# A five-stage graph network on one core: the three dense stages rewritten as one interleaved pass, with centred weights and a bias added by TensorE

## The chip, the cores and the metric

The kernel runs on one core of one Trainium2 chip. The metric is the device time of one execution in microseconds (us); lower is better. A difference is given against the median of the runs of the kernel before.

## What is computed

The reference chains two graph layers, a mixture of experts, a third graph layer and a block that modulates the better half of the tokens, on 6250 nodes with 256 features and 100000 edges, all in fp32:

```python
def _gnn_layer(x, row, col, W, b, g, beta):          # layers gnn0 and gnn1
    agg = segment_sum(x[col], row); deg = maximum(segment_sum(1, row), 1)
    h = (x + agg / deg) @ W.T + b
    mu = mean(h, -1); var = mean(square(h - mu), -1)
    return silu((h - mu) * rsqrt(var + EPS) * g + beta)

updated = x @ W_self.T + b_self + aggregate @ W_msg.T + b_msg     # layer gnn2
out = gelu(layernorm(updated) * ln_gamma + ln_beta)
```

After gnn1 and gnn2 the result is added to the residual `x`, and the sum is normalised again.

## The kernel before

The program is a list of stages, each a block in which the five engines have queues of their own and meet through semaphores; the next stage starts when all are through. The order is: `sort` (edges sorted by node through a table in DRAM), `sum0`, `gnn0`, `sum1`, `gnn1`, `route`, `moe_in`, `moe`, `moe_out`, `sum2`, `gnn2`, `half`. The nodes are held in SBUF as 49 tiles of 128 rows (NT = 49, D = 256, U = 7 tiles to a loop iteration, KB = 2 blocks of 128 columns): `p.acc` has the sums over edges and then the new rows, `p.xb` the rows before the layer.

`sum_over_edges` (L730) gathers the neighbours' rows by indirect DMAs on the POOL queue (L888) and adds them per node by one-hot matmuls (L956) and VectorE adds (L1118). In `sum2` it also makes `x @ W_self.T + b_self + b_msg` beside the gathers and puts it into `p.xb`.

`gnn_dense` (L1267) is the dense stage, built three times: `gnn0`, `gnn1` and `gnn2`. It has two passes over the 49 tiles. The first is class `Project` (L1132). Per tile VectorE makes the rows (`put`, L1280, a copy at L1282 in gnn2) four tiles ahead, TensorE transposes them with the identity (L1197, two matmuls) two tiles ahead, ScalarE copies the transposed rows out of PSUM (L1226), TensorE multiplies by the weights (L1212, two fp32 matmuls, which the trace shows as four records), VectorE adds the bias or `p.xb` on the way out of PSUM (`take`, L1286) and collects row statistics (`norm.take`, L568). Then `norm.finish` (L570 to L586) turns the statistics of all 49 tiles into mean and reciprocal deviation, with one square root by ScalarE (L629). The second pass is `tile` (L1325): per tile VectorE subtracts the mean and multiplies by gamma (`center`, L1315), multiplies by the deviation and adds beta (`scale`, L1321), ScalarE applies Silu or Gelu (L1366), and where there is a residual VectorE adds it (L1335) and takes the statistics of the sum (L568). Each loop iteration of ScalarE's second pass holds one ACT_TABLE_LOAD. In gnn0 the result is sent to DRAM by SyncE, seven tiles to a DMA (`send_steps`).

The edges' second table, which `sum2` reads, is written by 784 indirect DMAs on the POOL queue (`Scatter.run`, L1256). They are spread over three stages: columns 0 to 97 beside gnn0 (`EC // 8` = 98), 98 to 195 beside gnn1, and 196 to 783 beside `moe`. A stage that has scatters can't end before they are issued and landed.

Of the kernel before, what the change touches and what calls it, by code (L numbers as in the profile page):

```python
# [24 lines left out]
P = 128  # L25
N = 6250
D = 256
# [702 lines left out]
def sum_over_edges(p, source, order, weighted, table, own=None):  # L730
# [4 lines left out]
    with ExitStack() as ctx:  # L735
# [18 lines left out]
        s_landed, s_free = s("s_landed"), s("s_free")  # L754
        if own is not None:
# [82 lines left out]
        def _(act):  # L838
            if table is not None:
# [13 lines left out]
                clear(early, at)  # L853

# [407 lines left out]

def second_scatter(p, ctx):
    return Scatter(p, ctx, p.table1, p.addr1, p.rec1)


def gnn_dense(p, wk, mean_of_edges, row_bias, gamma, beta, func, residual, copy, scatters, left=None):  # L1267

    nc, v = p.nc, p.nc.vector
    with ExitStack() as ctx:
        deg = p.sb("g_deg", [P, NT], F32, ctx)
        norm, norm2 = RowNorm(p, ctx), left or RowNorm(p, ctx)

        def put(t, slots):
            a, x = flat(p.acc[:, bass.ds(t, 1), 0:D]), flat(p.xb[:, bass.ds(t, 1), :])
            if mean_of_edges:
                return [v.scalar_tensor_tensor(out=slots[0], in0=a, scalar=deg[:, bass.ds(t, 1)], in1=x,  # L1280
                                               op0=ALU.mult, op1=ALU.add)]
# [19 lines left out]
        block = ctx.enter_context(nc.Block())  # L1301

        @block.vector
        def _(dve):
# [16 lines left out]

            center(0, 0)
            center(1, 1)  # L1325
            scale(0, 0)

            def tile(t, u, more):
                x = flat(p.acc[:, bass.ds(t, 1), 0:D])
# [957 lines left out]
```

## Time and profile before

| what | us |
|---|---|
| three runs | 7439.2, 7442.39, 7440.92 (median 7440.92) |
| the profiled execution, its own time | 7400.07 |
| its span | 7398.1 |
| TensorE busy, share of the span | 49% |
| VectorE busy | 38% |
| ScalarE busy | 11% |
| GpSimd (POOL) busy | 51% |

In the profile PE is TensorE's matmuls, PEld its weight loads, DVE VectorE, ACT ScalarE, POOL GpSimd and SPq SyncE's queue. Times in the trace are microseconds from the span's start. A matmul in fp32 against the weights stands there as two records, a transposition as one. PEclk is the share of full speed that TensorE's clock was granted; 1.00 is 2.4 GHz and 0.50 is 1.2 GHz. The bracket at the end of a row of the timeline is how long the engine was idle before it, and what the profile gives as the releaser.

### The profile page before, as it was taken

To read this page: it belongs to the slowest core of one execution; us is meant where nothing else is said; L and a number is where in the kernel's file an instruction comes from. 1 tells how busy PE (TensorE), PEld (TensorE's weight loads), DVE (VectorE), ACT (ScalarE), POOL (GpSimd) and SP (SyncE) were. 2 spreads that over 40 slices of the span, in tenths; PEclk is the share of its full clock that TensorE was granted. 3 is DMA by queue.
4 is the path that set the end of the run, shared out by engine and by line. 5 is a ranking of instruction groups with operands and counts; after the bars stand their busy time and mean duration, and the time that the engine had idled before them with its cause. 6 is when DMAs were issued, how large, how long until landed. Compare 5 with 4: busy or idle time off the path is not lost. (4 is left out here: it accounts for less than half of the span.)

```text
span 7398.1 us, 63577 instructions
## 1 busy us (share of the span) xinstructions
PE 3606.4 (49%) x13693; PEld 2603.5 (35%) x13694; DVE 2823.8 (38%) x6837; ACT 831.4 (11%) x2066; POOL 3772.0 (51%) x3797
## 2 busy tenths in 40 slices
PE   4113965444433445445331222299992455555529
PEld 1001543333322333333230000078881344344317
DVE  5116854444435344444380000011114455555761
ACT  0001930000002000000130000022221100000222
POOL 4772046666662666666507777700005566667221
PEclk7556987777766777777655555599996777778759
DMA  3001023333311333332012000022214333333140
GB/s 134 1 0 37 13 58 92 93 92 91 92 42 47 92 91 93 92 93 84 5 38 91 2 4 4 9 72 81 81 57 135 90 91 92 90 90 92 55 160 18
DMA packets 290129, 497.38 MB, mean 67 GB/s; under 512 B 99253, under 2 KB 182880, under 8 KB 290048
## 3 DMA queue, kind: packets, MB, share of 16 engines
q0 software_dynamic: 163264, 345.19, 16.5%
q1 hardware_dynamic: 125696, 150.28, 6.3%
q10 hardware_dynamic: 1088, 1.05, 0.1%
q8 instruction: 25, 0.41, 0.0%
q14 instruction: 56, 0.46, 0.0%
HBM read 487.50 MB, written 92.89 MB: 78 GB/s over the span
## 5 line engine op out<-in xcount | busy, mean ns | idle before, releaser
L956 PE MATMUL sum_sums<-sum_got,sum_onehot 128*128 x4992 | 1627.4, 487 | 1717.5 <-DVE acc L1118 1317.3
L888 POOL DMA_INDIRECT sum_got<-xn,edge_row x1568 | 1539.5, 982 | 1139.8 <-issue 450.4
L956 PEld LDWEIGHTS sum_sums<-sum_got,sum_onehot 128*128 128x128 f32 x4992 | 1173.7, 245 | 2153.5 <-issue 1944.0
L1118 DVE TENSOR_TENSOR acc<-acc,sum_sums 128x257 f32 (+1 forms) x2496 | 1053.2, 422 | 1775.8 <-remote 1242.6
L888 POOL DMA_INDIRECT sum_got<-h,edge_row x784 | 753.9, 962 | 484.0 <-issue 226.3
L1256 POOL DMA_INDIRECT table<-rec,addr x784 | 807.8, 1030 | 291.5 <-issue 275.4
L1763 PE MATMUL moe_f_ps_y<-xb,moe_f_hT 128*128 128x256 f32 x1792 | 475.9, 398 | 297.7 <-issue 297.6
L1747 PE MATMUL moe_f_ps_h<-moe_f_xT,xb 128*128 128x256 f32 x1792 | 473.7, 398 | 286.5 <-issue 286.3
L1828 DVE TENSOR_TENSOR moe_f_y<-moe_f_ps_y,moe_b 128x256 f32<-128x256 f32 x112 | 42.3, 420 | 1337.2 <-PE moe_f_ps_y L1763 650.1
L1595 POOL DMA_INDIRECT moe_out_c_got<-moe_out,place_i x98 | 95.7, 976 | 826.2 <-PEq L1553 787.9
L1256 POOL DMA_INDIRECT table<-sort_rec,sort_addr x392 | 400.4, 1022 | 202.1 <-issue 122.5
L1763 PEld LDWEIGHTS moe_f_ps_y<-xb,moe_f_hT 128*128 128x128 f32 x1792 | 349.8, 197 | 391.6 <-issue 351.3
L1747 PEld LDWEIGHTS moe_f_ps_h<-moe_f_xT,xb 128*128 128x128 f32 x1792 | 352.9, 199 | 366.3 <-issue 324.7
L1075 DVE TENSOR_TENSOR sum_onehot<-iota,edge_local 128x512 f32<-128x512 f32 x636 | 435.4, 685 | 6.0 <-PEq L2246 6.0
L1795 ACT ACTIVATE moe_f_hT<-moe_f_ps_h,moe_b 128x256 f32<-128x256 f32 x448 | 187.9, 470 | 1365.4 <-remote 788.5
L310 PE MATMUL sort_placed<-acc 128*128 128x392 f16 x1576 | 264.1, 331 | 39.4 <-DVE acc L528 37.0
L1222 ACT ACTIVATE gnn_pr_spare<-eps 128x1 f32<-128x1 f32 x9 | 1.2, 193 | 2319.2 <-PEq L2246 2319.2
L252 ACT ACTIVATE acc<-acc,edge_row 128x128 f16<-128x128 f16 x784 | 256.2, 392 | 8.7 <-DVE acc L538 5.8
L1543 POOL DMA_INDIRECT moe_in<-xb,place_i x98 | 95.5, 975 | 257.2 <-DVE xb L609 227.6
L310 PEld LDWEIGHTS sort_placed<-acc 128*128 128x128 f16 x1576 | 154.6, 98 | 148.9 <-issue 39.3
L342 PE MATMUL sort_placed<-sort_mask,sort_before 128*128 128x392 f16 x168 | 68.6, 408 | 229.8 <-issue 149.8
L1197 PE MATMUL gnn_pr_psflip<-ident,gnn_pr_rows 128*128 128x128 f32 x294 | 67.1, 319 | 229.3 <-issue 137.4
(481 smaller groups left out, 3432.2 us busy)
## 6 DMA issues: line engine op xcount, KB each, us to landing
xb<-in_L_ffn_W SPq DMA_DIRECT2D x112, 1024.0 KB
sum_got<-xn,edge_row POOLq DMA_INDIRECT x1568
moe_in<-acc SPq DMA_DIRECT2D x28, 512.0 KB
moe_f_xin<-moe_in SPq DMA_DIRECT2D x56, 256.0 KB
moe_out<-moe_f_y SPq DMA_DIRECT2D x56, 256.0 KB
xn<-xb SPq DMA_DIRECT2D x14, 896.0 KB
table<-rec,addr POOLq DMA_INDIRECT x784
sum_got<-h,edge_row POOLq DMA_INDIRECT x784
```

Source lines behind the costliest of these rows:

```text
L252: nc.scalar.activation(hot[:, j, CH + part * P:CH + (part + 1) * P], hot[:, j, CH + 2 * P:CH + 3 * P], ACT.Copy, scale=value[:, bass.ds(n, ...
L310: mm = nc.tensor.matmul(placed[part][:, half, 0:CH // 2], hot[:, slot, CH + part * P:CH + (part + 1) * P], hot[:, slot, half * (CH // 2):( ...
L888: pool.indirect_dma_start(got[:, c % SU, 0:D], None, source, bass.IndirectOffsetOnAxis(ap=p.edge_row[:, c:c + 1], axis=0)).then_inc(s_got[ ...
L956: mm = nc.tensor.matmul(sums[k % 2][j], onehot[:, (k % QUARTERS) * HALF + j, :], flat(got[:, bass.ds(where[n % PLAN], 1), :]), start=True, ...
L1075: ins = v.tensor_tensor(out, number, local, ALU.is_equal)
L1118: v.tensor_tensor(a, a, sums[k % 2][j], ALU.add).then_inc(s_added[j], 1)
L1256: pool.indirect_dma_start(self.table, bass.IndirectOffsetOnAxis(ap=self.addr[:, c:c + 1], axis=0), self.rec[:, c, :], None, bounds_check=l ...
L1543: pool.indirect_dma_start(into[0:places, :], bass.IndirectOffsetOnAxis(ap=p.place_i[:, k, t:t + 1], axis=0), p.xb[:, t, :], None, bounds_c ...
L1595: pool.indirect_dma_start(got[:, t % U, k, :], None, source, bass.IndirectOffsetOnAxis(ap=p.place_i[:, k, t:t + 1], axis=0)).then_inc(s_go ...
L1747: mm = nc.tensor.matmul(ps_h[j // 2][:, j % 2, :], w1[:, wk, kb, j * P:(j + 1) * P], xT[:, k, kb, :], start=(kb == 0), stop=(kb == KB - 1))
L1763: mm = nc.tensor.matmul(ps_y[k][:, blk, :], hT[:, k, j, blk * P:(blk + 1) * P], w2[:, wk, j, :], start=False, stop=(j == HB - 1 and blk == 1))
L1795: nc.scalar.activation(hT[:, k, j, :], ps_h[j // 2][:, j % 2, :], func, bias=bias).then_inc(s_act, 1)
```

## The change

1. In `sum0` ScalarE, after it has cleared the sums, takes from each of the eight blocks of weights in `p.wT` and from four bias rows its mean over the 256 output columns (12 activations with an accumulated sum, one that divides by -256, and 12 that add the result). With centred weights and bias the projected row has mean zero. `sum1` and `sum2` have nothing of this.
2. `gnn_dense` is one interleaved pass, written out for all 49 tiles without loops. The bias row (gnn0, gnn1) or `p.xb` (gnn2) is added by TensorE: one more fp32 matmul per tile, with the identity as the weights and the row as the 256 moving columns. The variance comes from ScalarE, by a Square of the PSUM rows with scale 1/16 and an accumulated sum. VectorE's `center`, its first statistics and the copy of gnn2's rows are gone; its `take` multiplies by gamma. The square root is taken per group of seven tiles, and scale, activation and residual sum follow 9, 10 and 12 tiles behind.
3. The split of the scatters is 0 to 71 beside gnn0, 72 to 167 beside gnn1 and 168 to 783 beside `moe`.

```diff
+            for n, columns_of in enumerate(centre):
+                nc.scalar.activation(columns_of, columns_of, ACT.Copy, accum_out=middle[:, n:n + 1]).then_inc(s_totals, 1)
...
+            for n, columns_of in enumerate(centre):
+                nc.scalar.activation(columns_of, columns_of, ACT.Identity, bias=middle[:, n:n + 1]).then_inc(s_centred, 1)
...
+FEW, MOST = 72, 168
+BANKS, FLIPS, PUTS = 4, 2, 4
+SCALE_LAG, ACTIVE_LAG, SUM_LAG = 9, 10, 12
...
+        @block.tensor
...
+            for t in range(NT):
+                if t + FLIPS < NT:
+                    turn(t + FLIPS)
+                out = ps_out[t % BANKS][:, 0:D]
+                if t >= BANKS:
+                    pe.wait_ge(s_taken, t - BANKS + 1)
+                nc.tensor.matmul(out, p.ident[:], row_bias[:] if mean_of_edges else p.xb[:, t, :], start=True, stop=False)
+                pe.wait_ge(s_copied, t + 1)
+                for kb in range(KB):
+                    last = nc.tensor.matmul(out, flip[:, t % U, kb * P:(kb + 1) * P], p.wT[:, wk, kb, :], start=False,
+                                            stop=(kb == KB - 1))
+                last.then_inc(s_out, 1)
...
+        @block.scalar
...
+            for n in range(NT + ACTIVE_LAG):
+                if n + FLIPS < NT:
+                    keep(n + FLIPS)
+                if n < NT:
+                    act.wait_ge(s_out, n + 1)
+                    if n >= 2:
+                        act.wait_ge(s_square, n - 1)
+                    nc.scalar.activation(squares[:, n % 2, :], ps_out[n % BANKS][:, 0:D], ACT.Square, scale=1.0 / 16,
+                                         accum_out=std[:, n:n + 1]).then_inc(s_square, 1)
...
+                    nc.scalar.activation(out, scaled[:, t % U, :], func).then_inc(s_active, 1)
+                if n < NT and n % U == U - 1:
+                    act.wait_ge(s_square, n + 1)
+                    nc.scalar.activation(std[:, group(n // U)], std[:, group(n // U)], ACT.Sqrt,
+                                         bias=p.eps[:, 0:1]).then_inc(s_std, 1)
...
+        @block.vector
...
+            for n in range(NT + (SCALE_LAG if residual is None else SUM_LAG)):
+                if n < NT:
+                    dve.wait_ge(s_square, n + 1)
+                    v.tensor_tensor(p.acc[:, n, 0:D], ps_out[n % BANKS][:, 0:D], gamma[:], ALU.mult).then_inc(s_taken, 1)
+                    if mean_of_edges and n + PUTS < NT:
+                        put(n + PUTS)
...
-              row_params["L0_gnn_beta0"], ACT.Silu, None, dram["h1"], (0, EC // 8))
+              row_params["L0_gnn_beta0"], ACT.Silu, None, dram["h1"], (0, FEW))
-              row_params["L0_gnn_beta1"], ACT.Silu, io["x"], None, (EC // 8, EC // 4))
+              row_params["L0_gnn_beta1"], ACT.Silu, io["x"], None, (FEW, MOST))
-              (io["L0_ffn_W1"], io["L0_ffn_W2"], p.moe_b1, p.moe_b2), True, ACT.Gelu, (EC // 4, EC))
+              (io["L0_ffn_W1"], io["L0_ffn_W2"], p.moe_b1, p.moe_b2), True, ACT.Gelu, (MOST, EC))
```

TensorE's queue in gnn0, the first pass in the loop. Before, one tile is two transpositions (`psflip`) and two matmuls with the weights (`psout`); each `psout` row is two records of the trace:

```order
L1197 MATMUL gnn_pr_psflip<-ident,gnn_pr_rows 128x128
L1197 MATMUL gnn_pr_psflip<-ident,gnn_pr_rows 128x128
L1207 REGISTER_ALU
L1212 MATMUL gnn_pr_psout<-wT,gnn_pr_flip 128x256
L1212 MATMUL gnn_pr_psout<-wT,gnn_pr_flip 128x256
```

In the change it is:

```order
L1329 MATMUL gnn_g_psflip<-ident,gnn_g_mixed 128x128
L1329 MATMUL gnn_g_psflip<-ident,gnn_g_mixed 128x128
L1341 MATMUL gnn_g_psout<-row_L_gnn_b,ident 128x256
L1344 MATMUL gnn_g_psout<-wT,gnn_g_flip 128x256
L1344 MATMUL gnn_g_psout<-wT,gnn_g_flip 128x256
```

The third row, the bias times the identity, is new; it stands between the transposition two tiles ahead and the tile's own product.

ScalarE's queue in gnn0 of the change, around the end of a group of seven tiles (L1354 the copy of the transposed rows, L1365 the Square, L1376 Silu, L1379 the square root of a group):

```order
L1354 ACTIVATE gnn_g_flip<-gnn_g_psflip 128x256
L1365 ACTIVATE gnn_g_squares,gnn_g_std<-gnn_g_psout 128x256
L1376 ACTIVATE xb<-gnn_g_scaled 128x256
L1379 ACT_TABLE_LOAD
L1379 ACTIVATE gnn_g_std<-gnn_g_std,eps 128x7
L1354 ACTIVATE gnn_g_flip<-gnn_g_psflip 128x256
L1365 ACTIVATE gnn_g_squares,gnn_g_std<-gnn_g_psout 128x256
L1376 ACT_TABLE_LOAD
L1376 ACTIVATE xb<-gnn_g_scaled 128x256
```

Before, the copies, the root and Silu lay one after the other, with one table load per seven tiles; now they alternate, and a group has two.

VectorE's queue in gnn1, second pass before (one tile), and one step of the change (L1407 `take`, L1398 `put`, L1419 scale, L1425 the residual sum):

```order
L1321 SCALAR_TENSOR_TENSOR gnn_pr_flip<-gnn_g_centered,gnn_n6rstd,row_L_gnn_beta 128x256
L1335 TENSOR_TENSOR acc<-gnn_g_active,gnn_pr_rows 128x256
L1315 ISA
L1315 SCALAR_TENSOR_TENSOR gnn_g_centered<-acc,gnn_n6mean,row_L_gnn_g 128x256
L568 ISA
L568 BN_STATS gnn_n7stats<-acc 128x6
```

```order
L1407 TENSOR_TENSOR acc<-gnn_g_psout,row_L_gnn_g 128x256
L1398 SCALAR_TENSOR_TENSOR gnn_g_mixed<-acc,gnn_g_deg,xb 128x256
L1419 SCALAR_TENSOR_TENSOR gnn_g_scaled<-acc,gnn_g_std,row_L_gnn_beta 128x256
L1425 TENSOR_TENSOR acc<-gnn_g_active,gnn_g_old 128x256
L568 BN_STATS gnn_n5stats<-acc 128x6
```

The two passes together had seven operations per tile on this engine; the one step has five.

## Rows read from the trace of the kernel before

**Rows 1.** The page: the span

```profile
span 7398.1 us, 63577 instructions
```

**Rows 2.** Timeline: first instruction of gnn0, sum1, gnn1, route, gnn2 and half

```profile
2135.80 0.39 ACT L1222 ACTIVATE gnn_pr_spare<-eps 128x1 f32<-128x1 f32 x3 [1115.12 <-PEq L2246]
2380.64 0.69 DVE L1075 TENSOR_TENSOR sum_onehot<-iota,edge_local 128x512 f32<-128x512 f32 x1 [5.96 <-PEq L2246]
3515.86 0.39 ACT L1222 ACTIVATE gnn_pr_spare<-eps 128x1 f32<-128x1 f32 x3 [1140.64 <-PEq L2246]
3784.03 0.39 ACT L1222 ACTIVATE route_pr_spare<-eps 128x1 f32<-128x1 f32 x3 [0.93 <-PEq L2246]
6917.31 0.39 ACT L1222 ACTIVATE gnn_pr_spare<-eps 128x1 f32<-128x1 f32 x3 [63.42 <-PEq L2246]
7054.13 21.25 ACT L595 ACTIVATE xb<-acc,n2shift,n2rstd 128x256 f32<-128x256 f32 x43 [1.74 <-PEq L2246]
```

**Rows 3.** The scatters' line L1256 in gnn0 and in moe: ns min/median/max, first and last start

```profile
L1256 POOL DMA_INDIRECT table<-rec,addr x98: 971/972/1276, 2136.5 to 2261.5; - x98
...
L1256 POOL DMA_INDIRECT table<-rec,addr x588: 970/972/1799, 4006.4 to 4803.9; - x196
```

**Rows 4.** Windows: scatters in gnn0; gnn1 free of them; moe with; moe without

```profile
core 0: us, PE busy (x) PEld busy (x) DVE busy (x) ACT busy (x) POOL busy (x), PEclk, DMA share, GB/s
2180.00:2262.00 82.00, 11.98 (x30) 7.48 (x30) 5.77 (x15) 1.92 (x5) 62.51 (x65) 0.50 0.02 1
3660.00:3700.00 40.00, 34.41 (x181) 26.07 (x180) 38.39 (x106) 14.84 (x34) 0.00 (x0) 0.97 0.07 23
4400.00:4500.00 100.00, 20.34 (x36) 9.91 (x36) 1.75 (x4) 1.68 (x4) 77.94 (x71) 0.50 0.03 4
4950.00:5050.00 100.00, 100.00 (x470) 85.37 (x470) 10.66 (x25) 22.68 (x54) 0.00 (x0) 1.00 0.20 66
```

**Rows 5.** Timeline of VectorE's `take`, gnn0 during and after the scatters, and gnn1

```profile
2220.98 0.42 DVE L1286 TENSOR_TENSOR acc<-gnn_pr_psout,row_L_gnn_b 128x256 f32 x1 [15.65 <-DMA moe_out<-acc]
...
2274.25 0.43 DVE L1286 TENSOR_TENSOR acc<-gnn_pr_psout,row_L_gnn_b 128x256 f32 x1 [3.23 <-PE gnn_pr_psout L1212]
...
3654.32 0.43 DVE L1286 TENSOR_TENSOR acc<-gnn_pr_psout,row_L_gnn_b 128x256 f32 x1 [8.07 <-DMA moe_out<-acc]
```

**Rows 6.** Timeline of PE, first pass: one tile at 1.2 GHz, one at 2.4 GHz

```profile
2277.31 0.63 PE L1197 MATMUL gnn_pr_psflip<-ident,gnn_pr_rows 128*128 128x128 f32 x2
2279.44 0.63 PE L1197 MATMUL gnn_pr_psflip<-ident,gnn_pr_rows 128*128 128x128 f32 x2
...
6940.69 0.38 PE L1197 MATMUL gnn_pr_psflip<-ident,gnn_pr_rows 128*128 128x128 f32 x2
6941.77 0.39 PE L1197 MATMUL gnn_pr_psflip<-ident,gnn_pr_rows 128*128 128x128 f32 x2
```

**Rows 7.** Timeline of ScalarE in gnn1: root, table load, Silu

```profile
3696.88 0.34 ACT L629 ACTIVATE gnn_n6rstd<-gnn_n6var,eps 128x49 f32<-128x49 f32 x1 [3.33 <-DVE gnn_n6var L584]
3697.23 1.28 ACT L1366 ACT_TABLE_LOAD   x1
3699.06 0.81 ACT L1366 ACTIVATE gnn_g_active<-gnn_pr_flip 128x256 f32<-128x256 f32 x2 [0.54 <-DVE gnn_pr_flip L1321]
```

**Rows 8.** Timeline of VectorE in gnn1: `take` and `put`; one tile of the second pass

```profile
3659.86 0.42 DVE L1286 TENSOR_TENSOR acc<-gnn_pr_psout,row_L_gnn_b 128x256 f32 x1 [0.98 <-PE gnn_pr_psout L1212]
3660.20 0.47 DVE L1280 SCALAR_TENSOR_TENSOR gnn_pr_rows<-acc,gnn_g_deg,xb 128x256 f32 x1
...
3702.63 0.42 DVE L1335 TENSOR_TENSOR acc<-gnn_g_active,gnn_pr_rows 128x256 f32 x1
3702.96 0.48 DVE L1315 SCALAR_TENSOR_TENSOR gnn_g_centered<-acc,gnn_n6mean,row_L_gnn_g 128x256 f32<-128x256 f32 x1
3703.36 0.42 DVE L568 BATCH_NORM_STATS2 gnn_n7stats<-acc  x1
3704.08 0.42 DVE L1335 TENSOR_TENSOR acc<-gnn_g_active,gnn_pr_rows 128x256 f32 x1
```

More of the change, by code:

```diff
@@ L727, in at_least_one, with sum_over_edges @@
     return eng.snap(register, min_val=1, max_val=most)
-def sum_over_edges(p, source, order, weighted, table, own=None):
+def sum_over_edges(p, source, order, weighted, table, own=None, centre=()):
     nc, v = p.nc, p.nc.vector
@@ L1324, in _ @@
[L1324 to L1329, printed above, removed]
-                if more >= 1:
-                    scale(t + 1, (u + 1) % U)
-                dve.wait_ge(s_active, t + 1)
-                if residual is not None:
-                    dve.wait_ge(s_old[u], 16 * pr.i + 16)
-                    v.tensor_tensor(x, active[:, u, :], old[:, u, :], ALU.add).then_inc(s_summed, 1)
-                if more >= 2:
-                    center(t + 2, (u + 2) % U)
-                if residual is not None:
-                    dve.wait_ge(s_summed, t + 1)
-                    if u == 0:
-                        if isinstance(pr.i, int):
-                            c.leave(STEPS - 1)
-                        else:
-                            c.enter(pr.i, U)
-                    c.done(norm2.take(x, t))
@@ L1347, in _, with put @@
-            pr.steps(dve, tile)
+            def put(t):
+                if t >= U:
+                    dve.wait_ge(s_flip, t - U + 1)
+                v.scalar_tensor_tensor(out=mixed[:, t % U, :], in0=p.acc[:, t, 0:D], scalar=deg[:, t:t + 1],
+                                       in1=p.xb[:, t, :], op0=ALU.mult, op1=ALU.add).then_inc(s_put, 1)
+            if mean_of_edges:
+                for t in range(PUTS):
+                    put(t)
+            for n in range(NT + (SCALE_LAG if residual is None else SUM_LAG)):
[4 more added lines that the diff above has]
+                        put(n + PUTS)
+                if at_step(n, SCALE_LAG):
+                    t = n - SCALE_LAG
+                    if t % U == 0:
+                        dve.wait_ge(s_std, t // U + 1)
+                        v.reciprocal(std[:, group(t // U)], std[:, group(t // U)]).then_inc(s_rstd, 1)
+                        dve.wait_ge(s_rstd, t // U + 1)
+                        dve.wait_ge(s_taken, t + U)
+                    if t >= U:
+                        dve.wait_ge(s_active, t - U + 1)
+                    v.scalar_tensor_tensor(out=scaled[:, t % U, :], in0=p.acc[:, t, 0:D], scalar=std[:, t:t + 1], in1=beta[:],
+                                           op0=ALU.mult, op1=ALU.add).then_inc(s_scaled, 1)
+                if residual is not None and at_step(n, SUM_LAG):
+                    t = n - SUM_LAG
+                    dve.wait_ge(s_active, t + 1)
+                    dve.wait_ge(s_old[t % U], 16 * (t // U) + 16)
+                    v.tensor_tensor(p.acc[:, t, 0:D], active[:, t % U, :], old[:, t % U, :], ALU.add).then_inc(s_summed, 1)
+                    if t >= 1:
+                        dve.wait_ge(s_summed, t)
+                        c.done(norm2.take(p.acc[:, t - 1, 0:D], t - 1))
@@ L1348, in _ @@
             if residual is not None:
+                dve.wait_ge(s_summed, NT)
+                c.done(norm2.take(p.acc[:, NT - 1, 0:D], NT - 1))
                 c.settle()
```

128 lines of the change are left out of this document (70 added, 58 removed).

## The prediction

> **What bounds the kernel now.** I read the page for the span [rows 1], the timeline for where each dense stage begins and where the next stage takes over [rows 2], the scatters' line by stage [rows 3], windows of the stretches with and without scatters [rows 4], and then the timelines of the three engines that meet in a dense stage [rows 5 to 8]. The stages follow one another, so what a stage saves comes off the end. gnn0 lasts 2380.6 - 2135.8 = 244.8 us, gnn1 3784.0 - 3515.9 = 268.1 and gnn2 7054.1 - 6917.3 = 136.8 [rows 2], together 650 of 7398 us.
>
> The reader should see two regimes. While POOL issues scatters, TensorE gets through very few instructions: 30 matmul records in 82 us in gnn0 and 36 in 100 us in moe, against 470 in 100 us when moe is free of them [rows 4]. That is about 0.36 records per us in either stage, though their sizes differ. VectorE waits 15.65 us for each tile there [rows 5]. So a scatter is nearly serial time, wherever it stands. gnn0's dense work leaves this regime at 2274.25, 12.7 us after its last scatter starts (2261.5), and gnn1's at 3654.32 [rows 3, 5]. By then 15 tiles of either are through. The rest of gnn0 takes 2380.6 - 2274.3 = 106.4 us and that of gnn1 3784.0 - 3654.3 = 129.7; these, and the whole of gnn2, are two passes at engine speed: about 1.08 us a tile in the first, where TensorE sets the pace at full clock [rows 6], and 1.45 us a tile in the second of gnn1 and gnn2, all VectorE's (3702.63 to 3704.08) [rows 8].
>
> **The change part by part.** *Centring in sum0.* 25 short activations on ScalarE, at half a microsecond each 12 us at the most. ScalarE had been idle 1115.12 us before gnn0 [rows 2], beside the gathers. Nothing waits for it before gnn0: zero. Without that cover it would cost its 12 us.
>
> *Pace of the one pass.* TensorE: a tile costs 1.08 us at full clock [rows 6]; the identity matmul adds two records of 100 / 470 = 0.213 us [rows 4]: 1.51 us. ScalarE: two activations back to back span 0.81 us, so 0.39 from start to start [rows 7]; I take that for copy, Square and function, 1.17. A group of seven adds two table loads of 1.28 and a root of 0.34 [rows 7], 2.9 / 7 = 0.41. That makes 1.58. The trace of before has no ScalarE instruction with an accumulated sum; its extra lies between nothing and one more activation (0.39). VectorE in gnn0: take 0.34, put 0.40, scale 0.38, so 1.12. In gnn1 it also has the residual sum and statistics: 0.34 + 0.40 + (1.45 - 0.40 for the centring that goes, 3702.96 to 3703.36) = 1.79 [rows 8], with a reciprocal and waits per group 1.84. In gnn2 it has no put: 1.4. So gnn0 and gnn2 run at TensorE's and ScalarE's pace, and I take 1.6 us, nearest the sum of known rows; gnn1 runs at VectorE's, 1.84. Bounds for gnn0 and gnn2 are 1.51 and 2.1, the latter under the first rival.
>
> At this place the skill speaks against the change. The rows show a load of 1.28 us and at most 0.54 us between it and the next activation, which the profile gives to VectorE [rows 7]. The Trainium skill, page "ScalarE: Activation LUTs", section "What ACT_TABLE_LOAD costs", says that each switch to another set costs about 1.28 us of load and 1.38 us of drain, and wants calls batched by set; here a group has two switches. By that page, as an estimate, a tile costs 2 x 1.38 / 7 = 0.39 us more on ScalarE and the sum below ends near 7384 instead of 7353.
>
> *gnn0.* Scatters: 98 starts span 125.0 us, 1.289 each [rows 3]; 26 fewer end the slow regime 33.5 us earlier. In it TensorE did 15 x 4 + 17 x 2 = 94 records before; now it does 33.5 x 0.36 = 12 fewer, 82, and a tile has eight: (82 - 4 for the two turned ahead) / 8 = 9.7 tiles. 39.3 are left, x 1.6 = 62.9. The clock is at 1.2 GHz for the first 6 us or so, as before (a tile took 2.13 us there) [rows 6]: 3 more. After the last product ten lagging steps drain, with a root and a load: 7. Then the last rows go to DRAM, 6, as before [rows 2]. 78.9 instead of 106.4. Gain 33.5 + 27.5 = 61.0.
>
> *gnn1.* Two fewer scatters, 2.6. 93 records give 11.1 tiles; 37.9 are left, x 1.84 = 69.7, clock 3. The drain is nine steps at 1.05, three at 0.67 and 2 us for the root: 13.5. The normalisation of the sum stays: of the 129.7 us, 34 x 1.08 and 49 x 1.45 leave 22, less about 4 for the first pass's own statistics and root, which go [rows 7], so 18. Together 104.2. Gain 2.6 + 25.5 = 28.1.
>
> *gnn2.* No scatters. 3 to fill, 49 x 1.6 = 78.4, clock 2, drain 13.5, end 5: 101.9 against 136.8. Gain 34.9.
>
> *moe.* 28 more scatters, all beside moe. On average one took 797.5 / 587 = 1.36 us [rows 3], but in the late stretch 71 fit into 100 us [rows 4]; I take 1.39: 38.9 us, in which TensorE does 14 records that it need not do later, 3.0 us. Loss 35.9. At gnn0's 1.289 it would be 33.3.
>
> Sum: 61.0 + 28.1 + 34.9 - 35.9 = 88.1 us. The profiled execution's own time is 7400.1, so 7312 for that. It lies 0.55% under the median of the three runs, 7440.9; the prediction is for the median: 7440.9 - 88 = 7353. The other stages keep their instructions.
>
> **The rivals.** *ScalarE late.* If the accumulated Square costs a second step and each load drains, a tile costs 1.17 + 0.39 + (2 x (1.28 + 0.54) + 0.34) / 7 = 2.13. With 2.1: 88.3 tiles x 0.5 and 37.9 x 0.26 give 54 us back: 7407. For it: ScalarE goes from one operation at a time to three kinds in one queue, and a group's 2.9 us arrive in a lump while TensorE can run only about two tiles ahead. Against: four PSUM banks on each side cover about 3 us. The page named above is this rival's rule, at a smaller price.
>
> *TensorE's clock stays low.* The extra records cost double at 1.2 GHz. A tile took 2.13 us there [rows 6], so 2.13 + 2 x 0.426 = 2.98 now. Over all three stages: 39.3 x 1.38 + 37.9 x 1.14 + 49 x 1.38 = 165, less the 8 already counted: 7353 + 157 = 7510, 69 us slower than before. It decides in gnn0, gnn1 and gnn2 from the point where more than 88 / 157 = 56% of the tiles run low. Against: in gnn1's free stretch TensorE was busy 34.4 of 40 us and was granted 0.97 [rows 4]; in the change it would be busy at least 1.51 of 1.84.
>
> *A tile advances at its old rate beside the scatters.* If the slow regime counts tiles and not records, 13 and 15 tiles are through by its end instead of 9.7 and 11.1: 3.3 x 1.6 + 3.9 x 1.84 = 12.5 us more: 7340. Against: the equal record rate in moe and gnn0 [rows 4].
>
> *The change does not do what it says* in one respect already: 33.5 of gnn0's 61.0 us are moved scatters, which moe pays for. Their move alone is worth 33.5 + 2.6 - 35.9, nothing. If the interleaving failed as well, the time would be no change.
>
> **How the numbers follow.** Forecast 0.70, ScalarE late 0.13, tile rate 0.10, no change 0.02, low clock 0.05. The range reaches down to the tile-rate case with TensorE's bare 1.51 us (88.3 x 0.09 = 8 less) and the cheaper moe scatters (3 less), 7329, and some 15 us for the drains that I only estimated: 7314. Up it reaches towards ScalarE late: 7400. 0.2% is 15 us, about what a measurement of this kernel can tell from no change. Faster 0.93 (the first three cases), same 0.03, slower 0.04 (most of the low clock).
>
> **What would show it.** Right: gnn0 near 184 us, gnn1 near 240, gnn2 near 102, moe 36 us longer; in the free stretches takes 1.6 us apart in gnn0 and gnn2 and 1.84 in gnn1; eight records a tile at 0.36 records per us beside the scatters. Wrong: ScalarE without gaps and takes 2 us apart (first rival); a granted clock near 0.5 in the free stretches (second); 13 takes before gnn0's last scatter (third). If moe grows by less than 30 us, scatters there are partly hidden, and my serial reading of them fails.

## The result, and the profile after

| | us |
|---|---|
| before, four runs beside the change | 7440.06 (7438.15 to 7442.39) |
| the change, four runs | 7346.27 (7343.06 to 7351.86) |
| ratio, 95% interval | 0.9875 (0.9860 to 0.9889) |
| the profiled execution of the change, its own time | 7351.86, span 7349.8 |

The forecast was 7353 with a range of 7314 to 7400. The change saves 93.8 us where 88 were expected.

The page and the timeline of the change: its span, and the first rows of sum1, route, gnn2 and half, which answer to [rows 1, 2] (columns: start in us, duration, engine, line, operation, tiles, number, and in brackets the idle time before and its releaser). gnn1's first row on these engines is VectorE's at 3483.10.

```profile
span 7349.8 us, 62474 instructions
...
2335.26 0.69 DVE L1089 TENSOR_TENSOR sum_onehot<-iota,edge_local 128x512 f32<-128x512 f32 x1 [7.29 <-PEq L2298]
...
3719.67 0.39 ACT L1236 ACTIVATE route_pr_spare<-eps 128x1 f32<-128x1 f32 x3 [0.90 <-PEq L2298]
...
6904.87 1.51 PE L1329 MATMUL gnn_g_psflip<-ident,acc 128*128 128x128 f32 x6 [7.02 <-PEq L2298]
...
7005.56 1.58 ACT L595 ACTIVATE xb<-acc,n2shift,n2rstd 128x256 f32<-128x256 f32 x3 [1.72 <-PEq L2298]
```

With gnn0's own start at 2149.85, the stages of the two profiles, from the first row of one to the first row of the next (moe from VectorE's first row on its tokens, some 3 us into the stage, in both):

| stage | before | change | gain | forecast |
|---|---|---|---|---|
| gnn0 | 244.8 | 185.4 | 59.4 | 61.0 |
| gnn1 | 268.2 | 236.6 | 31.6 | 28.1 |
| gnn2 | 136.8 | 100.7 | 36.1 | 34.9 |
| moe | 1583.3 | 1621.3 | -38.0 | -35.9 |
| these four | 2233.1 | 2144.0 | 89.1 | 88.1 |
| sum0, sum1, sum2 | 3453.1 | 3490.1 | -37.0 | 0 |

The last line is not the change's: when it ran again (below) its sums took 1140, 1138 and 1172 us, as before, and the two kernels' medians differed by 93.2 us all the same. In this pair the profile of before lies 40 us under its own median and that of the change 6 us over its own, so the two profiles alone show a gain of only 48 us. A comparison of two single executions would have misled by half.

The scatters' line in gnn0 and in moe (durations in ns, first and last start), for [rows 3]:

```profile
L1270 POOL DMA_INDIRECT table<-rec,addr x72: 972/974/1252, 2150.6 to 2242.1; - x72
...
L1270 POOL DMA_INDIRECT table<-rec,addr x616: 970/974/1804, 3941.7 to 4777.8; - x154
```

Windows of the change: the later part of gnn0's scatters, its free stretch, gnn1's free stretch, moe with scatters, gnn2, for [rows 4]:

```profile
core 0: us, PE busy (x) PEld busy (x) DVE busy (x) ACT busy (x) POOL busy (x), PEclk, DMA share, GB/s
...
2200.00:2243.00 43.00, 6.50 (x16) 4.32 (x16) 1.63 (x4) 1.72 (x6) 32.94 (x34) 0.54 0.02 1
2256.00:2320.00 64.00, 56.77 (x280) 44.03 (x279) 42.45 (x109) 50.16 (x154) 0.00 (x0) 0.99 0.20 67
3620.00:3690.00 70.00, 62.94 (x281) 45.85 (x282) 63.48 (x178) 52.05 (x157) 0.00 (x0) 0.96 0.23 63
4400.00:4500.00 100.00, 21.03 (x36) 10.05 (x35) 1.75 (x4) 1.68 (x4) 76.87 (x72) 0.50 0.04 6
6915.00:6985.00 70.00, 67.67 (x346) 55.93 (x345) 53.10 (x151) 57.81 (x181) 0.00 (x0) 1.00 0.21 61
```

The reader should see three things. Beside scatters TensorE still gets through 16 records in 43 us and 36 in 100 us, the rate of before. In the free stretches it is granted 0.96 to 1.00, so it is at its 2.4 GHz level. And there TensorE is busy 89%, 90% and 97% of the three windows, ScalarE 74% to 83%, and in gnn1 VectorE 91%.

VectorE's `take` in gnn0 of the change: three beside scatters, and the eleventh, the first that comes at the free pace:

```profile
2190.22 0.42 DVE L1407 TENSOR_TENSOR acc<-gnn_g_psout,row_L_gnn_g 128x256 f32<-128x256 f32 x1 [14.72 <-issue]
...
2211.98 0.42 DVE L1407 TENSOR_TENSOR acc<-gnn_g_psout,row_L_gnn_g 128x256 f32<-128x256 f32 x1 [20.94 <-issue]
...
2234.41 0.42 DVE L1407 TENSOR_TENSOR acc<-gnn_g_psout,row_L_gnn_g 128x256 f32<-128x256 f32 x1 [21.61 <-issue]
...
2252.93 0.43 DVE L1407 TENSOR_TENSOR acc<-gnn_g_psout,row_L_gnn_g 128x256 f32<-128x256 f32 x1 [0.27 <-ACT gnn_g_squares L1365]
```

The first three are 22 us apart, eight records at 0.36 per us. The eleventh ends the slow stretch, as the fifteenth did before [rows 5].

ScalarE in gnn0 of the change, around the end of a group of seven:

```profile
2285.07 0.19 ACT L1365 ACTIVATION_READ_ACCUMULATOR gnn_g_squares<-gnn_g_psout 128x1 f32 x1
2285.17 0.41 ACT L1376 ACTIVATE xb<-gnn_g_scaled 128x256 f32<-128x256 f32 x1
2285.59 1.28 ACT L1379 ACT_TABLE_LOAD   x1
2286.89 0.30 ACT L1379 ACTIVATE gnn_g_std<-gnn_g_std,eps 128x7 f32<-128x7 f32 x1
2287.09 0.36 ACT L1354 ACTIVATE gnn_g_flip<-gnn_g_psflip 128x256 f32<-128x256 f32 x1
2287.36 0.38 ACT L1365 ACTIVATE gnn_g_squares<-gnn_g_psout 128x256 f32<-128x256 f32 x1
2287.62 0.20 ACT L1365 ACTIVATION_READ_ACCUMULATOR gnn_g_squares<-gnn_g_psout 128x1 f32 x1
2287.84 1.28 ACT L1376 ACT_TABLE_LOAD   x1
2289.13 0.42 ACT L1376 ACTIVATE xb<-gnn_g_scaled 128x256 f32<-128x256 f32 x1
```

The activation behind a load starts as the load ends (2285.59 + 1.28 = 2286.87 and 2286.89; 2287.84 + 1.28 = 2289.12 and 2289.13), and the load starts as the activation ahead of it ends. The accumulated sum has a row of its own, 0.2 us, of which about 0.1 shows in ScalarE's pace.

### The profile page after: what moved, and what is told of

It reads as the page before. It is cut to its first block and busy times, and to the rows that moved or that the text cites. A ratio compares the mean times of both kernels' runs of the same rounds, so it can differ in the third digit from the quotient of the medians.

```text
span 7349.8 us, 62474 instructions
## 1 busy us (share of the span) xinstructions
PE 3665.0 (50%) x13987; PEld 2653.6 (36%) x13988; DVE 2691.0 (37%) x6479; ACT 911.7 (12%) x2424; POOL 3773.9 (51%) x3797
## 5 line engine op out<-in xcount | busy, mean ns | idle before, releaser
L1354 ACT ACTIVATE gnn_g_flip<-gnn_g_psflip 128x256 f32<-128x256 f32 x147 | 54.8, 373 | 2379.7 <-PE gnn_g_psflip L1329 2332.3
L1344 PE MATMUL gnn_g_psout<-wT,gnn_g_flip 128*128 128x256 f32 x588 | 167.0, 410 | 2.3 <-ACT gnn_g_flip L1354 2.3
```

Of the source, the lines that this page charges most:

```text
L1344: last = nc.tensor.matmul(out, flip[:, t % U, kb * P:(kb + 1) * P], p.wT[:, wk, kb, :], start=False, stop=(kb == KB - 1))
```

## The experiments

The time of a kernel here depends on the chip that it met. Every comparison is with runs of the kernel before on the same chip, and the stages of two profiles are compared only where both come from one chip. The first eight experiments ran on one chip (before: 7401.12 and 7400.43), the next three on a second (before: 5656.65), the last on a third (before: 5642.56). What sets these apart is itself a finding, told with experiment 11.

| run | median us | ratio to before (95%) | gnn0 | gnn1 | gnn2 | moe |
|---|---|---|---|---|---|---|
| 1 before again | 7401.5 | | 243.9 | 268.0 | 136.3 | 1582.7 |
| 2 split 98, 196 | 7302.6 | 0.9869 (0.9852 to 0.9885) | 214.0 | 235.9 | 101.2 | 1583.2 |
| 3 split 150, 300 | 7306.3 | 0.9871 (0.9854 to 0.9887) | 284.7 | 303.8 | 101.4 | 1449.1 |
| 4 split 49, 98 | 7306.7 | 0.9871 (0.9854 to 0.9887) | 155.7 | 175.8 | 100.5 | 1711.2 |
| 5 the change again | 7307.2 | 0.9875 (0.9860 to 0.9891) | 183.9 | 236.1 | 99.9 | 1620.9 |
| 6 no table switches | 7282.9 | 0.9844 (0.9828 to 0.9859) | 173.1 | 229.0 | 93.7 | 1621.6 |
| 7 no identity matmul | 7282.5 | 0.9837 (0.9822 to 0.9853) | 176.8 | 227.2 | 95.0 | 1619.8 |
| 8 turn three ahead | 7403.8 | 1.0004 (0.9995 to 1.0014) | 235.9 | 278.1 | 101.3 | 1620.0 |
| 9 turn three, put six | 5574.3 | 0.9857 (0.9840 to 0.9873) | 104.4 | 144.7 | 100.3 | 837.3 |
| 10 put six | 5575.8 | 0.9861 (0.9845 to 0.9878) | 105.4 | 144.8 | 100.6 | 837.9 |
| 11 no centring | 5584.2 | 0.9873 (0.9856 to 0.9889) | 108.5 | 144.1 | 100.0 | 838.5 |
| 12 put six, split 98, 196 | 5608.5 | 0.9941 (0.9927 to 0.9955) | 139.7 | 147.0 | 100.9 | 837.2 |

**1. The kernel before again.** No edit.

> The kernel before, profiled once more. The two profiles differ by 48 us of span while the medians differ by 94 us. In the profile of before the three gather stages sum0, sum1 and sum2 are 14.0, 12.6 and 11.1 us shorter than in that of the change. Theory: that is a difference between two executions or chips, not the change; a second profile of the same kernel has sum1 near 1147 us (1135.2 in the first) and a time near 7440. Rival: the change itself lengthens the gathers; then this profile has sum1 at 1135 again.

It took 7401.53 us, and the kernel before beside it 7401.12: 39 us less than in the result's runs. sum1 took 1138.2 us. That is nearer the rival's 1135 than the theory's 1147, and the time isn't near 7440 either. But the rival, that the change lengthens the gathers, falls with run 5. So a level of some 40 us belongs to the chip or the hour and not to a kernel; on this chip the change is as much lower (7307 against 7346). It lies in the sums: the first profile of the change has 39.8 us more in the three of them than run 5.

**2 to 4. The split of the scatters alone.** The change with

```diff
-FEW, MOST = 72, 168
+FEW, MOST = 98, 196      # 2; in 3: 150, 300; in 4: 49, 98
```

> The change with the scatters split as before (98, 98, 588 instead of 72, 96, 616). Theory that scatters are nearly serial wherever they stand: gnn0 31 us longer (33.5 of scatters less 1.5 tiles at 1.82), gnn1 2 longer, moe 35 shorter (28 x 1.36 less 3): 7344, the same as the change within 5 us. Rival, the new split is part of the gain: over 15 us slower than the change.

> The change with the split 150, 150, 484. Theory: gnn0 +92 (78 x 1.289 less 4.5 tiles at 1.82), gnn1 +63, moe -169, since scatters issued more than 200 us after the first of a stage take 1.39 and not 1.29 us each: 14 us faster than the change, 7332. Rival, moe hides a part of its scatters: then moe loses less than 150 us and the whole is slower than the change.

> The change with the split 49, 49, 686: fewest scatters beside the dense stages. Theory: gnn0 -27, gnn1 -55, moe +88 to +92: 6 to 10 us slower than the change. Rival, moe hides a part of its scatters: over 10 us faster than the change.

All three have the ratio of the change within its interval. The stages move by a lot, the sum hardly: gnn0, gnn1 and moe together take 2033 us at 98 and 196, 2038 at 150 and 300, 2041 with the change's own split (run 5), 2043 at 49 and 98. A scatter that is moved takes its 1.1 to 1.4 us along: from run 2 to run 3, 52 more in gnn0 cost 70.7 us (1.36 each), 52 more in gnn1 67.9 (1.31), and 104 fewer in moe save 134.1 (1.29). That is the serial reading of the scatters, confirmed on this chip. Neither the saving of 14 us that I had expected of the wide split nor the loss of 6 to 10 us of the narrow one is there.

**5. The change again**, unedited, beside the next three.

> The change itself again, on the chip of this group of runs, as the reference for the three beside it. The stage lengths should be 185 (gnn0), 237 (gnn1), 101 (gnn2) and 1621 (moe). Theory A (a scatter costs the same wherever it stands): it is level with the version split at 98 and 196, ratio near 0.987. Theory B (28 scatters cost 38 us in moe's late stretch and gave only some 28 in gnn0): its ratio is 0.9882, about 9 us more than the version split at 98 and 196 had in the group before. The three sum stages should show whether the 14, 13 and 11 us by which they were longer in the first profile of the change belong to it (then they come again) or to that execution (then they are 1145, 1138 and 1173, as in the kernel before).

7307.23 us, ratio 0.9875, the very ratio of the result. Theory B's 9 us aren't excluded: it came out 4.6 us over run 2, in another group of runs, and the intervals overlap. The sums took 1140.3, 1138.4 and 1171.6 us, so what they had more in the first profile isn't the change's. Against run 1, gnn0 gains 60.0, gnn1 31.9, gnn2 36.4 and moe loses 38.2: 90.1 in all.

**6. No table switches.** The group's root is replaced by an activation that needs no table but the stage's own; this leaves out the square root of the variance.

```diff
-                    nc.scalar.activation(std[:, group(n // U)], std[:, group(n // U)], ACT.Sqrt,
+                    nc.scalar.activation(std[:, group(n // U)], std[:, group(n // U)], ACT.Identity,
                                          bias=p.eps[:, 0:1]).then_inc(s_std, 1)
```

> The group's square root is left out (the statistics pass through unchanged by an Identity), so ScalarE needs no table but one in each dense stage. Theory A (the two table loads and the root of a group of seven are only partly covered, because TensorE can run about two tiles ahead): the takes of gnn0's free stretch come 1.51 to 1.55 us apart on average instead of 1.82, those of gnn1 1.84 instead of 1.96, those of gnn2 1.51 instead of 1.66; with the drain's own root gone that is 12 + 5 + 6 + 3, some 25 us less than the change. Rival (the group's 2.9 us are covered and the pace is lost to the semaphores between the engines): under 5 us.

24.4 us less than run 5, where 25 were expected: 10.8 in gnn0, 7.1 in gnn1 and 6.2 in gnn2. Windows of the free stretches of this run (gnn0, gnn1, gnn2):

```profile
core 0: us, PE busy (x) PEld busy (x) DVE busy (x) ACT busy (x) POOL busy (x), PEclk, DMA share, GB/s
2238.00:2290.00 52.00, 52.00 (x266) 40.77 (x265) 40.74 (x104) 35.68 (x136) 0.00 (x0) 1.00 0.22 72
3590.00:3640.00 50.00, 47.98 (x223) 34.27 (x223) 49.86 (x143) 31.14 (x115) 0.00 (x0) 1.00 0.26 74
6865.00:6910.00 45.00, 45.00 (x240) 38.94 (x239) 44.32 (x124) 31.86 (x123) 0.00 (x0) 1.00 0.31 88
```

Now TensorE is busy all the time in gnn0 and gnn2, at 1.58 and 1.52 us a tile, and VectorE in gnn1, at 1.82. The prediction had worked out 1.51 for TensorE and 1.84 for VectorE; why gnn0 stays 0.06 over gnn2 isn't shown. The two loads and the root of a group are thus only partly hidden.

**7. No identity matmul.** This leaves out the bias rows of gnn0 and gnn1 and, in gnn2, the nodes' own projection.

```diff
-                nc.tensor.matmul(out, p.ident[:], row_bias[:] if mean_of_edges else p.xb[:, t, :], start=True, stop=False)
...
-                    last = nc.tensor.matmul(out, flip[:, t % U, kb * P:(kb + 1) * P], p.wT[:, wk, kb, :], start=False,
+                    last = nc.tensor.matmul(out, flip[:, t % U, kb * P:(kb + 1) * P], p.wT[:, wk, kb, :], start=(kb == 0),
                                             stop=(kb == KB - 1))
```

> The matmul with the identity is left out, and with it the bias row of gnn0 and gnn1 and, in gnn2, the nodes' own projection. Theory A (beside scatters TensorE gets through a fixed number of records): a tile has six records instead of eight, the takes come 16.8 us apart instead of 22.4, 13 tiles are through when gnn0's slow regime ends and 15 or 16 in gnn1. Beyond that ScalarE with its loads (some 1.6 us a tile) and, in gnn1, VectorE (1.84) set the pace, so gnn0 gains 3.6 x 1.82 + 36 x 0.2, some 14 us, gnn1 about 7, gnn2 at most 3: 20 to 25 us less than the change. Rival 1 (a tile costs 22 us there whatever its records): the takes stay 22.4 us apart and the gain is under 10. Rival 2 (TensorE sets the pace in the free stretches): gnn0 and gnn2 fall by a further 0.3 us a tile, to 1.3, 40 us less in all.

24.8 us less than run 5 by the medians, 20.9 by the three stages. VectorE's take in gnn0 beside scatters, in this run:

```profile
2198.75 0.43 DVE L1406 TENSOR_TENSOR acc<-gnn_g_psout,row_L_gnn_g 128x256 f32<-128x256 f32 x1 [15.29 <-issue]
...
2215.55 0.42 DVE L1406 TENSOR_TENSOR acc<-gnn_g_psout,row_L_gnn_g 128x256 f32<-128x256 f32 x1 [15.59 <-issue]
...
2232.35 0.42 DVE L1406 TENSOR_TENSOR acc<-gnn_g_psout,row_L_gnn_g 128x256 f32<-128x256 f32 x1 [15.59 <-issue]
```

They are 16.80 us apart, to the hundredth what six records at 0.357 per us make; the tile-rate rival is dead, the count of records rules. Windows of the same run (gnn0 beside scatters; the free stretches of gnn0 and of gnn2):

```profile
core 0: us, PE busy (x) PEld busy (x) DVE busy (x) ACT busy (x) POOL busy (x), PEclk, DMA share, GB/s
2170.00:2232.00 62.00, 9.12 (x24) 5.52 (x22) 3.89 (x10) 5.12 (x14) 46.16 (x47) 0.50 0.02 1
2255.00:2298.00 43.00, 32.66 (x144) 23.25 (x144) 28.71 (x75) 34.83 (x108) 0.00 (x0) 0.90 0.25 84
6875.00:6920.00 45.00, 34.22 (x167) 26.18 (x165) 38.67 (x112) 39.07 (x120) 0.00 (x0) 1.00 0.27 79
```

TensorE falls to 76% busy, yet gnn2's tiles still come 1.67 us apart once the lagging steps run, as with the identity, and gnn0's 1.68 to 1.88. Rival 2 fails too: TensorE isn't the only bound. ScalarE with its loads stands right beside it (87% busy in the last row). So taking the identity away alone gives nothing in gnn2 once the lagging steps run (nearly all of its 4.9 us comes from the first eleven tiles, 1.09 us apart instead of 1.51) and at most 0.14 us a tile in gnn0, while taking the loads away (run 6) gave 0.14 to 0.24 us a tile. The rest of gnn0's and gnn1's gain here comes from beside the scatters.

**8. Turned three ahead.**

```diff
-BANKS, FLIPS, PUTS = 4, 2, 4
+BANKS, FLIPS, PUTS = 4, 3, 4
```

> TensorE turns, and ScalarE copies, one tile further ahead (three instead of two). Theory A (the lump of loads is uncovered because TensorE runs out of copied tiles): it has one more tile of 1.5 us at each lump, so up to 1.5 us less at each of about 16 lumps in the free stretches: 10 to 20 us less than the change. Rival (the lump is uncovered because the Squares of the tiles in PSUM come late, and takes and banks with them): no difference, within 3 us.

In this line FLIPS is how many tiles ahead TensorE turns (transposes), and PUTS how many ahead VectorE makes the mixed rows that are turned. Both theories miss: 96.6 us more than run 5, and the whole gain of the change gone. It is lost in gnn0 (52) and gnn1 (42), while gnn2, which makes no mixed rows, is 1.4 us from run 5. TensorE and VectorE in gnn0 of this run, two tiles each:

```profile
2281.56 0.44 PE L1329 MATMUL gnn_g_psflip<-ident,gnn_g_mixed 128*128 128x128 f32 x2 [1.42 <-DVE gnn_g_mixed L1398]
2281.83 0.60 PE L1341 MATMUL gnn_g_psout<-row_L_gnn_b,ident 128*128 128x256 f32 x2
2282.26 1.03 PE L1344 MATMUL gnn_g_psout<-wT,gnn_g_flip 128*128 128x256 f32 x4
2284.71 0.44 PE L1329 MATMUL gnn_g_psflip<-ident,gnn_g_mixed 128*128 128x128 f32 x2 [1.42 <-DVE gnn_g_mixed L1398]
```

```profile
2280.68 0.42 DVE L1407 TENSOR_TENSOR acc<-gnn_g_psout,row_L_gnn_g 128x256 f32<-128x256 f32 x1 [1.94 <-ACT gnn_g_squares L1365]
2281.03 0.47 DVE L1398 SCALAR_TENSOR_TENSOR gnn_g_mixed<-acc,gnn_g_deg,xb 128x256 f32<-128x256 f32 x1
2281.42 0.48 DVE L1419 SCALAR_TENSOR_TENSOR gnn_g_scaled<-acc,gnn_g_std,row_L_gnn_beta 128x256 f32<-128x256 f32 x1
2283.83 0.42 DVE L1407 TENSOR_TENSOR acc<-gnn_g_psout,row_L_gnn_g 128x256 f32<-128x256 f32 x1 [1.94 <-ACT gnn_g_squares L1365]
```

A ring has closed. Before it multiplies tile t, TensorE turns tile t + 3; its mixed row is put by VectorE behind the take of tile t - 1; that take waits for ScalarE's Square of tile t - 1, which waits for TensorE's product of t - 1. So product, Square, take, put, turn and product follow one another at 3.15 us a tile, and each of the engines idles for the others. The distance that counts is PUTS less FLIPS: at 2 the ring spans two tiles and is loose, at 1 it is tight.

**9 and 10. Mixed rows six tiles ahead.**

```diff
-BANKS, FLIPS, PUTS = 4, 2, 4
+BANKS, FLIPS, PUTS = 4, 3, 6      # 9; in 10: 4, 2, 6
```

> As the run that turned three tiles ahead, but VectorE also makes the mixed rows six tiles ahead instead of four. Theory A (that run lost 52 us in gnn0 and 42 in gnn1 because the mixed row of the tile to be turned was made only after the take of the tile just multiplied, so the engines worked one after another, 3.15 us a tile): with six ahead the loop is open again, gnn0 is at 184 us or under and gnn1 at 236 or under, and gnn2, which makes no mixed rows, stays at 100. If a share of the uncovered loads in gnn0 and gnn1 comes from the same short lead, each group of seven there falls from 12.7 and 13.7 us towards gnn2's 11.6 and the floor of VectorE: up to 6 us less in either. Rival (three tiles ahead is itself the trouble, by the banks of PSUM): gnn0 stays over 220.

> The change with the mixed rows made six tiles ahead instead of four, nothing else. Theory A (part of the gap between gnn0's 12.7 us a group and gnn2's 11.6 is TensorE waiting for mixed rows behind the lump of table loads): gnn0 178 to 183 and gnn1 230 to 235 us, some 5 to 10 us less than the change in all. Rival (two tiles of lead are enough and the gap is VectorE's own work): no difference, within 3 us.

The runs met the second chip, so gnn0's length can't be held against 184 us. What can be compared is the pace. A group of seven in gnn0's even stretch takes 11.1 us in both, against 12.7 us in run 11, on the same chip with the change's own 2 and 4 (there the same two takes stand at 1675.23 and 1687.97; on the first chip it is 12.7 too). VectorE's take seven tiles apart, in run 10:

```profile
1670.33 0.42 DVE L1407 TENSOR_TENSOR acc<-gnn_g_psout,row_L_gnn_g 128x256 f32<-128x256 f32 x1 [1.52 <-ACT gnn_g_squares L1365]
...
1681.46 0.42 DVE L1407 TENSOR_TENSOR acc<-gnn_g_psout,row_L_gnn_g 128x256 f32<-128x256 f32 x1 [1.52 <-ACT gnn_g_squares L1365]
```

Turning three ahead is thus not a trouble in itself, and it brings nothing either: two or three, 5574.3 or 5575.8 us. Part of gnn0's uncovered load was TensorE waiting for mixed rows, which the change's own profile shows once one looks for it. TensorE in gnn0 of run 5, the two turns behind a pair of loads:

```profile
2257.71 0.44 PE L1329 MATMUL gnn_g_psflip<-ident,gnn_g_mixed 128*128 128x128 f32 x2 [0.81 <-DVE gnn_g_mixed L1398]
...
2260.07 0.44 PE L1329 MATMUL gnn_g_psflip<-ident,gnn_g_mixed 128*128 128x128 f32 x2 [0.63 <-DVE gnn_g_mixed L1398]
```

0.81 + 0.63 = 1.44 us is most of the 1.6 us a group that six ahead takes away. In gnn1 it gives nothing in the even stretch: a group takes 13.7 us with four ahead and with six. In gnn0 as a whole three to four us are gained; more can't be had there on this chip, since VectorE then waits some 20 us at the stage's end for the 72 scatters (the row stands with run 12). gnn1 ends in the same way here, which its length of 144.8 us (144.1 in run 11) hides. In run 10, gnn1's scatters and VectorE's first row of route:

```profile
L1270 POOL DMA_INDIRECT table<-rec,addr x96: 971/980/1612, 2735.6 to 2868.6; - x96
...
2879.76 0.09 DVE L1180 MEMSET route_pr_spare<- 128x1 f32 x2 [25.74 <-PEq L2298]
```

gnn1's dense work is over after 120 us, and the stage then waits 25 us for its 96 scatters. Run 10 is 8.4 us under run 11 by the medians; the intervals of the ratios overlap, and of the difference between the two profiles only 3.1 us lie in gnn0, so as a whole-kernel gain it isn't shown, only as a pace.

**11. No centring in sum0**; this leaves out that the weights' and bias rows' means are taken away.

```diff
-        stage("sum0", sum_over_edges, dram["xn"], 0, False, dram["table0"], None, centre)
+        stage("sum0", sum_over_edges, dram["xn"], 0, False, dram["table0"])
```

> The centring of weights and bias rows in sum0 is left out, so gnn0, gnn1 and gnn2 normalise rows whose mean isn't taken away. Theory A (centring lies beside the gathers and costs nothing): the same time as the change, ratio near 0.987, sum0 at 1140 to 1145 us. Rival (sum0 waits for ScalarE): sum0 and the time 12 us less.

sum0 took 1016.4 us, and 1015.2 and 1016.6 in runs 9 and 10, which do centre. So centring costs nothing there, whichever chip: on the first one too sum0 was at 1144.8 in run 1 without it and at 1140.3 in run 5 with it. The other half of the expectation, sum0 at 1140 to 1145, fell with the chip.

That chip is the surprise. Windows of run 11 in gnn0 and in moe, both beside scatters:

```profile
core 0: us, PE busy (x) PEld busy (x) DVE busy (x) ACT busy (x) POOL busy (x), PEclk, DMA share, GB/s
1620.00:1720.00 100.00, 80.09 (x392) 62.17 (x392) 61.21 (x156) 70.35 (x216) 74.57 (x72) 0.95 0.21 62
3500.00:3600.00 100.00, 100.00 (x468) 85.37 (x468) 10.51 (x24) 22.72 (x55) 76.22 (x79) 1.00 0.29 88
```

The last row has 79 scatters and 468 matmul records in 100 us; on the chip of the result a stretch of moe beside scatters has 72 of them and 36 records, and 470 only without scatters [rows 4]. The slow stretch on which the whole of the prediction turned does not exist here. moe takes 838 us instead of 1621, sort 604 instead of 993, each sum some 120 us less; gnn2 and route, which have no scatters, take what they take there (100.0 and 86.0 us). And the change is worth the same 1.3% (72 us in run 11). It must be made up otherwise: here the dense work of gnn0 and gnn1 runs at full pace beside the scatters, and it is the stage's end that waits for them, 14 us in gnn0 and 23 in gnn1 of run 11. How the 72 us divide by stage isn't shown, as the kernel before has no profile on this kind of chip.

**12. Six ahead, with the old split.**

```diff
-FEW, MOST = 72, 168
+FEW, MOST = 98, 196
-BANKS, FLIPS, PUTS = 4, 2, 4
+BANKS, FLIPS, PUTS = 4, 2, 6
```

> The mixed rows six tiles ahead, and the scatters split at 98 and 196 as in the kernel before. The last three runs were on a chip whose TensorE isn't held back beside scatters (468 records in 100 us of moe with 79 scatters, before near 5657 us), the runs before them on one where it is (36 records, before near 7400). What the split is worth should depend on that. On a chip that holds TensorE back (before near 7400): level with the first version split at 98 and 196, ratio 0.986 to 0.987, gnn0 at 208 to 214 us. On one that doesn't (before near 5657): gnn0 has to wait for its 98 scatters of 1.277 us, 125 us and their landing, so it takes 130 us or more instead of 105, gnn1 is level at 145 (its 98 scatters take 125), moe is level at 838 (588 scatters take 751): 25 us more than with 72 and 168, 5600, ratio near 0.990. Rival (the split is worth nothing on either): 5575 there.

The third chip is of the second kind too. The ratio is 0.9941, that of run 10 0.9861: 0.8%, some 45 us by the ratios, where 25 were expected. gnn0 took 139.7 us instead of 105.4 and gnn1 2.2 more; moe took 837.2 instead of 837.9 with 28 scatters fewer. That is 36 us; the rest I can't place, and the chips differ. gnn1's 98 scatters took 135.0 us there and not the 125 expected, so gnn1 waits for them too. In this run, the scatters' line in gnn0 and VectorE's first row of sum1, and then the same two of run 10:

```profile
L1270 POOL DMA_INDIRECT table<-rec,addr x98: 971/972/1278, 1621.2 to 1748.8; - x98
...
1760.17 0.69 DVE L1089 TENSOR_TENSOR sum_onehot<-iota,edge_local 128x512 f32<-128x512 f32 x1 [53.83 <-PEq L2298]
```

```profile
L1270 POOL DMA_INDIRECT table<-rec,addr x72: 971/972/1279, 1620.7 to 1716.0; - x72
...
1725.34 0.69 DVE L1089 TENSOR_TENSOR sum_onehot<-iota,edge_local 128x512 f32<-128x512 f32 x1 [19.94 <-PEq L2298]
```

In run 12 VectorE is idle 53.8 us at gnn0's end: its work ended at 1706, 86 us after the stage's start, and the 98 scatters last 127.6 us. The shorter gnn0 of the change needs fewer scatters beside it on this kind of chip. The change's third part, which is worth nothing on the first kind, is there worth about half of the gain (36 us by the stages, of 81 in run 10). moe took 837 to 838 us with 588 scatters and with 616, so there more could be moved to it from gnn0 and above all from gnn1, for some 12 and 24 us as an estimate (the waits of run 10, 19.9 and 24.9, less the 7.3 and 0.9 that the same two stage ends have in the profile of the change); no run tried it.

No run showed a version that beats the change beyond its interval. Six ahead (run 10) is the likeliest: it has the better pace in gnn0 and lies 8 us under run 11 on the second chip. On the first kind of chip it wasn't run.

## Why the prediction was right

*Beside scatters.* The reading of the slow stretch as a rate of records was right, to about a tile, in every number that could be tested on this kind of chip: takes 22 us apart, gnn0's slow stretch over 103.1 us after its start where 104.9 were put, and with it the eleventh tile, where 9.7 were worked out; run 7 adds the 16.8 us of six records. In gnn1 twelve tiles were through instead of 11.1, 136.3 us after its start where 135.9 were put. Scatters are serial wherever they stand (runs 2 to 4). But the prediction took this for a property of the chip, and it is one of some chips.

*Pace.* This step was off. gnn0 was put at 1.6 us a tile; the profile has 12.7 us for seven tiles, 1.82. gnn2 was put at 1.6 and took 1.51 until the lagging steps begin and 1.67 after; gnn1 was put at 1.84 and took 1.96. I had spread a group's two loads and root over seven tiles (0.41 each) and compared ScalarE's sum with TensorE's, as if the larger of two averages were the pace. The lump of 2.9 us (two loads and a root) is only partly covered by the lead of two tiles: between lumps a tile takes 1.5 us, at them two tiles take 2.4 to 2.6 each. Run 6 measured it: the switches cost 10.8, 7.1 and 6.2 us in the three stages, and the bare paces under them are 1.58, 1.82 and 1.52, where 1.51, 1.84 and 1.51 were worked out. In gnn0 the excess over 1.6 was TensorE waiting, behind the lump, for mixed rows: with them six ahead a tile takes 1.59 us, loads and all (runs 9 and 10, on the second chip).

*Why the sum still held.* In gnn0 the slow stretch ended 1.8 us sooner than put, and the rest took 3.4 us more: 82.3 (2252.93 to 2335.26) against 78.9. The 38 takes still to come after the eleventh take 70.0 us, to 2323.0, 4.1 more than the 65.9 put for them: 8.3 more by the pace (38 x 0.219), 2.1 less because 1.3 tiles fewer were left, 0.8 less for the slow clock (0.50 was granted until 2256, and the first seven takes needed 2.2 us more than seven do later, where 3 were put), and 1.3 less at the quicker end. The drain and the last rows took 12.3 instead of 13. In gnn1 the takes needed 72.5 us where 72.7 were put (37 at 1.96, the slow start with them, for 37.9 at 1.84 and the clock), and drain and normalisation 27.8 instead of 31.5. In gnn2 4.7 to fill, 78.9 for the takes and 17.1 for the rest stand against 3, 80.4 and 18.5. So the failed step, the pace, was an error of 8 us in gnn0 and 4 in gnn1, and small errors of the other sign, the clock, the tiles left and the drains, took it back. That they did so is luck.

*moe.* 28 scatters made their run 836.0 us long instead of 797.5 and the stage 38.0 us longer, 1.36 each, the stretch's mean [rows 3]; I had taken 38.9. The 3.0 us that I gave back for TensorE's records didn't come.

*Centring.* Zero, as put (run 11).

*The rivals.* Of ScalarE late the lump came true, that a group's loads arrive together while TensorE runs only two tiles ahead, at a little under half of its price per tile (0.22 of 0.5 us in gnn0, 0.12 of 0.26 in gnn1). Its other condition, that each load drains, did not. The rule of the Trainium skill, page "ScalarE: Activation LUTs", section "What ACT_TABLE_LOAD costs", was weighed there. Here the load of 1.28 us is as that section says, but the 1.38 us of drain that it adds to each switch doesn't show: the rows leave 0.01 and 0.02 us between a load and what is around it. By that page, as an estimate, the prediction put 7384; added up again (88.3 tiles x 0.37 and 37.9 x 0.13, on 7353) it is 7391, against 7346 measured. The clock was granted at 0.96 to 1.00 in the free stretches but for their first microseconds, so the low-clock rival had nothing for it. Tiles beside scatters slowed with their records, so the tile-rate rival had nothing either.

*What it rested on.* The forecast was for the median, 7440.9, though it used a profile at 7400. That was sound, as the 40 us proved to be a level that both kernels share.

## What to carry to other kernels

Where a lump of work on one engine recurs, work out the lead that covers it and every ring of waits through it; the average load per tile only bounds the pace from below. When one look-ahead is lengthened, check those that feed it: what counts is the difference between them, and one tile too little cost here all that the rewrite had gained. How a queue of small DMAs shares the chip with the dense work must be measured on more than one chip before a split is tuned to it: the same split was worth nothing on one kind and about half of the gain on the other, where both stages still ended in a wait for their scatters.

## What the runs showed of the hardware

Chips differ in what indirect scatters do to TensorE. On the chip of runs 1 to 8, as on that of the result, TensorE runs 36 matmul records in 100 us beside them, one in 2.8 us, whatever its work; each takes 0.59 us at the 1.2 GHz level and the gap has no releaser. TensorE in moe of the kernel before:

```profile
4442.54 0.58 PE L1763 MATMUL moe_f_ps_y<-xb,moe_f_hT 128*128 128x256 f32 x1 [2.21 <-issue]
4445.35 0.59 PE L1763 MATMUL moe_f_ps_y<-xb,moe_f_hT 128*128 128x256 f32 x1 [2.23 <-issue]
```

On the chips of runs 9 to 12 TensorE isn't slowed beside them at all: 468 records in 100 us of moe, and 12.7 us for seven tiles in gnn0 as without scatters. The scatters come there every 1.28 us in moe, 1.32 to 1.34 in gnn0 and 1.39 to 1.40 in gnn1, on the first kind every 1.36 in moe and 1.28 to 1.29 in gnn0 and gnn1 with the split of the change. The kernel before takes 7400 us on the one kind and 5650 on the other. Beside gathers the kinds lie nearer together: 162 records beside 70 gathers in 100 us of sum0 in the kernel before, 174 beside 80 in run 11. What makes the difference isn't shown: two of the chips were met for one group of runs each, so it may be the chip or something else that changed with it, and no run here varied the scatters' size or their destination.
